# A decoder layer on one core: centred weights, heads on row halves, and low parts of the keys on GpSimd

## What is computed

```python
q, k, v = (x @ Wq.T), (x @ Wk.T), (x @ Wv.T)        # 16 heads of 16 features
mu = q.mean(-1); var = ((q - mu) ** 2).mean(-1)      # over the 16 features of a head; k alike
qn = (q - mu) / sqrt(var + 1e-5) * gamma + beta      # k alike
phi = [qn*qn / 4, sqrt(2/16) * qn_i * qn_j (i<j)]    # so phi_q . phi_k = (qn . kn / 4) ** 2
y = causal_sum(phi_q.phi_k * v) / (causal_sum(phi_q.phi_k) + 1e-5)
x = layernorm(x + y @ Wo.T)
```

## Time and profile before

| | us |
|---|---|
| median of 3 runs (lowest, highest) | 1490.67 (1488.88, 1492.04) |
| the profiled execution, its own time | 1501.86 |
| its span | 1500.1 |
| PE, DVE, POOL, ACT busy in the span | 1243.3, 754.2, 684.5, 582.5 |
| mean granted TensorE clock, share of full speed | 0.899 |

### The profile page before, as it was taken

The page is one execution under the profiler, slowest core; times in us unless marked ns, Lnnn a source line. Parts: engine busy times, 40 slices in busy tenths (PEclk is TensorE's granted clock), DMA queues, the critical chain, the costliest instruction groups (busy, mean ns, idle before and its releaser), DMA issues.

```text
span 1500.1 us, 20297 instructions
## 1 busy us (share of the span) xinstructions
PE 1243.3 (83%) x6416; PEld 712.3 (47%) x6416; DVE 754.2 (50%) x1328; ACT 582.5 (39%) x999; POOL 684.5 (46%) x597
## 2 busy tenths in 40 slices
PE   3488778856999899998999989999994449999970
PEld 3355454534554445544455444554543426666640
DVE  6475858536335753458624665446423432222217
ACT  3364555632444544445434444444441012222210
POOL 0132323420467674676655766666794431111111
PEclk8688897966999999999999999999996569999995
DMA  5580000010000100000000000000002921111113
GB/s 172 197 270 16 1 0 0 1 45 11 1 0 1 36 10 1 1 1 23 22 2 1 1 11 23 1 0 1 1 1 83 316 68 42 44 46 42 45 43 143
DMA packets 33007, 64.66 MB, mean 43 GB/s; under 512 B 4221, under 2 KB 22398, under 8 KB 32640
## 3 DMA queue, kind: packets, MB, share of 16 engines
q1 hardware_dynamic: 23200, 32.41, 6.6%
q10 hardware_dynamic: 6304, 22.59, 4.7%
q0 software_dynamic: 3408, 8.43, 1.6%
HBM read 52.89 MB, written 28.34 MB: 54 GB/s over the span
## 4 chain that ended last, share of the span: by engine, by line
PE 60%; DVE 20%; issue 10%; ACT 3%; POOL 2%; DMA 2%; another core or an unknown queue 1%; ACTq 1%; SPq 0%; DVEq 0%; POOLq 0%
PE PS L1582 11%; PE PS L1689 9%; PE PS L1510 9%; PE PS L1593 8%; DVE mxp L1168 5%; PE PS L1706 5%; PE PS L225 3%; PE PS L1417 2%; PE PS L1523 2%; PE PS L226 2%; PE PS L227 2%; DVE R L1148 2%; PE PS L1406 2%; PE PS L1427 2%; POOL acc L608 1%
## 5 line engine op out<-in xcount | busy, mean ns | idle before, releaser
L608 POOL TENSOR_TENSOR acc<-acc,PX 128x1024 f32<-128x1024 f32 (+1 forms) x176 | 421.2, 2393 | 161.1 <-ACT PX L846 155.2
L846 ACT ACTIVATE PX<-PS 128x1024 f32<-128x1024 f32 (+1 forms) x208 | 212.9, 1025 | 247.2 <-PE PS L1582 236.4
L1168 DVE TENSOR_REDUCE mxp<-PS 128x2 f32<-128x804 f32 x256 | 240.4, 986 | 132.3 <-PE PS L1523 131.9
L1593 PE MATMUL PS<-PX,V 128*64 128x512 f32 (+1 forms) x832 | 226.3, 623 | 0.0
L550 POOL TENSOR_SCALAR_AFFINE_SELECT A<-A 128x128 f32<-128x128 f32 x256 | 88.8, 359 | 219.8 <-ACT A L751 216.2
L1689 PE MATMUL PS<-W,XBT 128*128 x312 | 149.6, 603 | 1.3 <-ACT XBT L902 1.3
L751 ACT ACTIVATE A<-PS 128x512 f32<-128x512 f32 (+3 forms) x256 | 99.3, 437 | 98.0 <-PE PS L1417 90.9
L669 POOL DMA_INDIRECT Y<-yb,goal_u x39 | 38.4, 986 | 201.8 <-DVE yb L1327 196.7
L1417 PE MATMUL PS<-qT,kT 128*128 128x512 f32 (+3 forms) x256 | 88.0, 420 | 27.0 <-ACT A L751 21.9
L1582 PEld LDWEIGHTS PS<-QH,KH 64*128 64x128 f32 (+1 forms) x416 | 38.4, 181 | 151.3 <-issue 89.9
L1582 PE MATMUL PS<-QH,KH 64*128 64x512 f32 (+1 forms) x416 | 104.6, 499 | 3.5 <-issue 2.2
(11 more groups left out here) (261 smaller groups left out, 2138.9 us busy)
## 6 DMA issues: line engine op xcount, KB each, us to landing
W<-in_w SPq DMA_DIRECT2D x24, 512.0 KB
XB<-XG ACTq DMA_DIRECT2D x39, 129.0 KB, 2.1
yl<-Y SPq DMA_DIRECT2D x4, 1024.0 KB, 9.0
X<-in_x SPq DMA_DIRECT2D x1, 2048.0 KB, 12.1
out<-X SPq DMA_DIRECT2D x4, 512.0 KB, 2.9
xt_raw<-in_xt SPq DMA_DIRECT2D x3, 512.0 KB, 4.4
c_raw<-in_ctxt SPq DMA_DIRECT2D x6, 200.0 KB, 2.4
c_raw<-in_ctxt SPq DMA_DIRECT2D x12, 100.0 KB, 2.6
```

The source lines that it names most:

```text
L608: ins = pool.tensor_tensor(sums[0:r], sums[0:r], PX[0:r, (NL * p + t) % NP, :, :], ALU.add)
L846: act.activation(PX[0:r, u % NP, :, :], PS[0:r, score_buffer(u):score_buffer(u) + 2, :], ACT.Exp, scale=XD ** -0.5)\
L1168: dve.tensor_reduce(mxp[:, p % 2, :, v % NT, v // NT:v // NT + 1].rearrange("p a o -> p (a o)"), PS[:, k:k + 2, 0:BW], AX, ALU.max)\
L1593: mm = pe.matmul(PS[rows, 4, :], V[0:LROWS[j], j, P * p + XD * half:P * p + XD * half + XD], PX[0:LROWS[j], u % NP, half, :], start=(j == ...
```

## The change

1. The weights of q and k are centred once, in `raw`, before they are split: per head of 16 features the mean over the columns is taken off (DVE), so the projections come out centred and `centre` is gone from DVE. ACT squares straight from PSUM, and `normalise` reads PSUM and writes `cen`. Bank 2 is free only after `normalise` (`nrm_ok`). In the opening, odd blocks use bank 6.
2. `kT` holds two heads on 128 rows. A turn is one copy of 128x512, not two of 64x512. Scores are made in pairs: head 2m from rows 0 to 63, head 2m+1 from rows 64 to 127, into banks 4 and 5; ACT squares both in one instruction, and the next pair waits for that instruction. The memsets of `kT` are gone.
3. POOL makes the low parts of the keys; DVE keeps those of the queries.
4. Variance moves up to the slot of the squares, normalise and affine one slot earlier. On PE both projections of a block stand behind the slot's value products. The opening takes blocks in pairs.

```diff
-            for i in range(NT):
-                for after, kind in ((1, "project v"), (1, "project qk"), (2, "centre"), (3, "variance"), (4, "normalise"), (5, "affine")):
+            for i in reversed(range(NT)):
+                for after, kind in ((1, "project v"), (1, "project qk"), (2, "variance"), (2, "centre"), (3, "normalise"), (4, "affine")):
                     ahead.setdefault(2 * i + after, []).insert(0, (kind, i))
...
-        OPENING = [("x",)] + [(kind, 0) for kind in FEATURES[0:3]]
-        for i in range(NT):
-            OPENING += [(kind, i + 1) for kind in FEATURES[0:3] if i + 1 < NT] + [(kind, i) for kind in FEATURES[3:]] \
-                + ([("split", i - 1)] if i >= 1 else [])
-        OPENING += [("split", NT - 1)] + [("vs", g) for g in range(3)] \
+        OPENING = [("x",)]
+        for two in ((0, 1), (2, 3)):
+            OPENING += [(kind, i) for i in two for kind in FEATURES[0:3]] + [("variance", i) for i in two]
+            OPENING += [("split", i - 2) for i in two if i >= 2]
+            OPENING += [("normalise", i) for i in two] + [("affine", i) for i in two]
+        OPENING += [("split", i) for i in (2, 3)]
+        OPENING += [("vs", g) for g in range(3)] \
...
+                if s[0] == "split":
+                    i = s[1]
+                    k = feat[:, i, D:].rearrange("p (h f) -> p h f", f=SF)
+                    pool.wait_ge(hi_ok, 8 * b + 2 * i + 2)
+                    pool.tensor_tensor(KX[:, i, :, 1:4:2, :], k.unsqueeze(2).broadcast_to([P, SH, 2, SF]),
+                                       as32(KX[:, i, :, 0:4:2, :]), ALU.subtract).then_inc(lo_ok, 1)
...
-                act.wait_ge(cen_ok, NT * t + i + 1)
-                act.activation(feat[:, i, :], cen[:, i % 2, :], ACT.Square).then_inc(sq_ok, 1)
+                act.wait_ge(qk_mm, NT * t + i + 1)
+                act.activation(feat[:, i, :], bank(qk_bank(t, i)), ACT.Square).then_inc(sq_ok, 1)
...
-                for j in range(4):
-                    u, c = 4 * n + j, n % NT
-                    act.wait_ge(sc_mm, 64 * b + u + 1)
+                for two in range(2):
+                    u, c = 4 * n + 2 * two, n % NT
+                    act.wait_ge(sc_mm, 64 * b + u + 2)
...
-                    act.activation(A[:, u % 8, P * c:T], PS[:, 4 + u % 2, P * c:T], ACT.Square,
-                                   scale=0.25).then_inc(sqr_ok, 1)
+                    act.activation(A[:, u % 8:u % 8 + 2, P * c:T], PS[:, 4:6, P * c:T], ACT.Square,
+                                   scale=0.25).then_inc(sqr_ok, 2)
...
+            dve.wait_ge(ld_q, 16)
+            for c in range(KC):
+                ins = dve.tensor_reduce(w_mean[:, c, :], groups[c], AX, ALU.add)
+            ins.then_inc(wch, 1)
+            dve.wait_ge(wch, 1)
+            dve.tensor_scalar(w_mean[:, :, :], w_mean[:, :, :], -1.0 / SF, None, ALU.mult).then_inc(wch, 1)
+            dve.wait_ge(wch, 2)
+            for c in range(KC):
+                ins = dve.tensor_tensor(groups[c], groups[c], w_mean[:, c, :].unsqueeze(2).broadcast_to([P, 32, SF]), ALU.add)
...
-                chain(dve.tensor_reduce(g_mean[:, i % 2, :], v, AX, ALU.add), cch, at + 1)
-                chain(dve.tensor_scalar(g_mean[:, i % 2, :], g_mean[:, i % 2, :], -1.0 / SF, None, ALU.mult), cch, at + 2)
-                if wait:
-                    dve.wait_ge(feat_ok, NT * t + i - 1)
-                dve.tensor_tensor(cen[:, i % 2, :].rearrange("p (g f) -> p g f", f=SF), v,
-                                  g_mean[:, i % 2, :].unsqueeze(2).broadcast_to([P, 32, SF]), ALU.add).then_inc(cen_ok, 1)
...
-                dve.tensor_copy(kT[0:64, g % 2, 2 * q, :], bank(1, rows=64)).then_inc(kT_ok, 1)
-                dve.tensor_copy(kT[64:P, g % 2, 2 * q + 1, :], PS[64:P, 1, :]).then_inc(kT_ok, 1)
+                dve.tensor_copy(kT[:, g % 2, q, :], bank(1)).then_inc(kT_ok, 1)
...
-                if started(t, i, 1):
-                    pe.wait_ge(cen_ok, NT * t + i)
+                if isinstance(t, int) and t == 0:
+                    if i >= 2:
+                        pe.wait_ge(nrm_ok, i - 1)
+                else:
+                    pe.wait_ge(nrm_ok, NT * t + i)
...
-                if started(b, u, 2):
-                    pe.wait_ge(sqr_ok, 64 * b + u - 1)
-                pe.matmul(PS[:, 4 + u % 2, P * c:T], kT[:, g % 2, j, P * c:P * c + P],
-                          qT[:, g % 2, j // 2, P * c:T], start=True, stop=True).then_inc(sc_mm, 1)
+                if started(b, u, 2):
+                    pe.wait_ge(sqr_ok, 64 * b + u)
+                for half in range(2):
+                    rows = slice(64 * half, 64 * half + 64)
+                    pe.matmul(PS[:, 4 + half, P * c:T], kT[rows, g % 2, two, P * c:P * c + P],
+                              qT[rows, g % 2, two, P * c:T], start=True, stop=True).then_inc(sc_mm, 1)
...
-                    half = (len(steps) + 1) // 2
-                    for j in range(4):
+                    steps.sort(key=lambda ds: ds[1][0] in ("project qk", "project v"))
+                    half = min((len(steps) + 1) // 2, sum(s[0] not in ("project qk", "project v") for d, s in steps))
+                    for two in range(2):
```

More of the change, by code:

```diff
@@ L678, in _ @@
             act.dma_start(xt_raw[:, :, :], xt[0].rearrange("(c p) t -> p c t", p=P)).then_inc(ld_xt, 16)
-            act.wait_ge(ld_q, 16)
-            act.copy(WSh[:, :, 0:3 * D], raw[:, 0:2, 0:3 * D]).then_inc(w_hi, 1)
             def x_high(t):
@@ L765, in _ @@
                 if s == ("x",):
+                    act.wait_ge(wch, 3)
+                    act.copy(WSh[:, :, 0:3 * D], raw[:, 0:2, 0:3 * D]).then_inc(w_hi, 1)
                     act.wait_ge(ld_w, 16 * N_LDW)
@@ L934, in _ @@
             dve.memset(VS[:, :, :, SF:], 1.0).then_inc(const_dve, 1)
-            dve.memset(as32(kT[64:P, :, 0:4:2, :]), 0.0).then_inc(const_dve, 1)
-            dve.memset(as32(kT[0:64, :, 1:4:2, :]), 0.0).then_inc(const_dve, 1)
+            groups = [raw[:, c, 0:2 * D].rearrange("p (g f) -> p g f", f=SF) for c in range(KC)]
+            dve.wait_ge(ld_q, 16)
[7 more added lines that the diff above has]
+                ins = dve.tensor_tensor(groups[c], groups[c], w_mean[:, c, :].unsqueeze(2).broadcast_to([P, 32, SF]), ALU.add)
+            ins.then_inc(wch, 1)
+            dve.wait_ge(wch, 3)
             dve.wait_ge(w_hi, 1)
@@ L979, in normalise @@
                 v = cen[:, i % 2, :].rearrange("p (g f) -> p g f", f=SF)
-                dve.tensor_tensor(v, v, rs.unsqueeze(2).broadcast_to([P, 32, SF]), ALU.mult).then_inc(nrm_ok, 1)
+                if started(t, i, 2):
+                    dve.wait_ge(feat_ok, NT * t + i - 1)
+                dve.tensor_tensor(v, bank(qk_bank(t, i)).rearrange("p (g f) -> p g f", f=SF), rs.unsqueeze(2).broadcast_to([P, 32, SF]), ALU.mult).then_inc(nrm_ok, 1)
             def affine(t, i):
@@ L1373, in _ @@
             pe.wait_ge(const_pool, 3)
-            pe.wait_ge(const_dve, 3)
+            pe.wait_ge(const_dve, 1)
             pe.wait_ge(w_lo, 1)
@@ L1396, in project_v, with turn @@
                 mm.then_inc(v_mm, 1)
-            def turn(b, g, q, src, bk, done, free, per):
+            def turn(b, g, q, src, bk, done, free):
                 h = 4 * g + 2 * q
@@ L1403, in turn @@
                 if started(b, 2 * g + q, 1):
-                    pe.wait_ge(free, per * (8 * b + 2 * g + q))
+                    pe.wait_ge(free, 8 * b + 2 * g + q)
                 for i in range(NT):
@@ L1408, in turn, with scores @@
                 mm.then_inc(done, 1)
-            def score(b, n, j):
-                g, c, u = n // NT, n % NT, 4 * n + j
-                if c == 0 and j == 0:
+            def scores(b, n, two):
+                g, c, u = n // NT, n % NT, 4 * n + 2 * two
+                if c == 0 and two == 0:
                     pe.wait_ge(qT_ok, 8 * b + 2 * g + 2)
-                    pe.wait_ge(kT_ok, 16 * b + 4 * g + 4)
+                    pe.wait_ge(kT_ok, 8 * b + 2 * g + 2)
                 if started(b, u, 2):
-                    pe.wait_ge(sqr_ok, 64 * b + u - 1)
-                pe.matmul(PS[:, 4 + u % 2, P * c:T], kT[:, g % 2, j, P * c:P * c + P],
-                          qT[:, g % 2, j // 2, P * c:T], start=True, stop=True).then_inc(sc_mm, 1)
+                    pe.wait_ge(sqr_ok, 64 * b + u)
[3 more added lines that the diff above has]
+                              qT[rows, g % 2, two, P * c:T], start=True, stop=True).then_inc(sc_mm, 1)
             def value(b, n, j):
@@ L1448, in step @@
                 if kind == "turn q":
-                    turn(b, s[1], s[2], QX, 0, tq_mm, qT_ok, 1)
+                    turn(b, s[1], s[2], QX, 0, tq_mm, qT_ok)
                 if kind == "turn k":
-                    turn(b, s[1], s[2], KX, 1, tk_mm, kT_ok, 2)
+                    turn(b, s[1], s[2], KX, 1, tk_mm, kT_ok)
                 if kind == "back":
@@ L1476, in attention @@
```

(15 more changed lines are left out.)

23 lines of the change are left out of this document (8 added, 15 removed).

## The result

| | before | with the change |
|---|---|---|
| median, us (lowest, highest), 4 runs each | 1489.78 (1486.94, 1492.04) | 1528.97 (1523.49, 1531.24) |
| profiled execution, own time (span) | 1501.86 (1500.1) | 1523.49 (1521.7) |
| DVE, ACT, POOL busy | 754.2, 582.5, 684.5 | 701.6, 572.2, 693.6 |

The ratio is 1.0259, 95% interval [1.0225, 1.0292]: **slower by 39 us**, where 1496.5 was forecast with a range up to 1509. The sign was the one that held most of the chance; the size is out by a factor of over six.

A forecast was written before the change was run, and what follows sets the result against it. No engine was full; PE's waits in a ring of hand-overs bound the self-attention. Opening -1.5, batch 0 +1.9, loop batches +7.0 and batch 3 -1.5 gave +5.9 on the profiled 1501.9, carried over to 1496.5 us; range 1475 to 1509.

The forecast's parts named there:

- The sum, batch 2 at full clock: Self-attention batch 2, added by stretches of slots: 69.3 us, 2.3 less than before; with low clock 75.1, 3.5 more.
- Low keys on POOL: Slots 9 to 12: subtraction takes 1.3 us, masks come 1.3 to 2 later, all but about 1 us a batch hidden.
- Scores in pairs: Self-attention scores: PE's score work halves, paired rounds cost 1.02 us of square plus 0.6 latency; batch 3 gains 1.5.
- the waits for bank 2: PE in slots 3, 5 and 7 waits for normalise before the next projection: 3.1, 3.2 and 4.1 us.
- The lower clock behind them: Projections after those waits run at half clock: 1.75 us more each, 5.8 a loop batch with half an output projection.
- The opening: Before the first batch: PE starts at 14, first turn comes at 46.6 instead of 48.09, saving 1.5 us.
- what would show it: Right: nine 3 to 4 us waits, lower clock, batches 73 or more. Wrong: slots 10 to 13 waiting over 1 for masks.
- POOL is slow: Rival, 0.10: POOL's low part takes 2.6 us and delays masks; +6 to +12 on top, 1502 to 1509.
- the root on ACT: Slots 3, 5, 7: ACT takes the previous block's root only after its squares, then DVE's chain takes 1.9 us.
- The clock holds: Rival, 0.28: projections of slots 3, 5 and 7 run at 2.4 GHz; loop batches win 2.3 each, 1480.
- Waits cancel: Rival, 0.16: ACT reaches its root earlier, each batch loses 2 us less of waiting; 1491.
- Row halves bring nothing: Rival, 0.03: paired 64-row score matmuls are drained or run in series; +18 on top, 1514.

The follow-up runs named there:

- r2: The changed kernel, but DVE copies the projection to `cen` at once, freeing bank 2 early; square and normalise read the copy: 1494.57 us, ratio 1.0031.
- r8: The kernel before with row halves alone (one `kT` copy a turn, 64-row scores), each head squared singly: 1488.01 us, ratio 0.9991.
- r5: r4 with the low keys back on DVE: 1472.41 us, ratio 0.9893 to the kernel before.
- r1: The changed kernel with the low keys on DVE again, behind those of the queries: 1517.87 us, ratio 1.0182 to the kernel before.
- r6: The kernel before with the low keys on POOL and nothing else changed: 1500.57 us, ratio 1.009.
- r4: The changed kernel with the edits of r2 and r3 together: 1481.06 us, ratio 0.9939 to the kernel before.
- r3: The changed kernel, row halves kept, but each head scored and squared by itself in two banks by turns: 1515.11 us, ratio 1.017.
- r16: r5 run again unchanged, on the chip of the job of r13 and r14: 1472.36 us, ratio 0.989 to the kernel before.
- r7: The changed kernel with ACT taking the root ahead of the squares of its slot: 1538.44 us, ratio 1.0343 to the kernel before.
- r9: r7 with DVE also normalising ahead of the copy of a finished group: 1513.88 us, ratio 1.0109 to the kernel before.
- r13: r16 plus POOL's low-key subtraction on spare buffers, same shape and place, result unused: 1491.63 us, ratio 1.0032 to the kernel before.
- r14: r16 plus five masks of 128x128 on a spare buffer at the subtraction's place on POOL: 1488.05 us, ratio 1.0004 to the kernel before.
- r10: r4 with POOL's low-key subtraction behind the masks of the next slot: 1490.48 us, ratio 0.9932 to the kernel before.

## Why the prediction was right and wrong

In short: the waits came as forecast, and the forecast failed in what it set against them and in two costs that it put near nothing. The steps that failed are the 69.3 us of "The sum, batch 2 at full clock", the 1 us a batch of "Low keys on POOL", and the -1.5 of batch 3 by "Scores in pairs".

**Right: the waits for bank 2.** Nine, of 2.94, 3.04 and 3.98 us in batch 1 against 3.1, 3.2 and 4.1; in batch 0, 3.06, 2.20 and 3.06. The lower clock behind them, and its price per projection (1.55 to 1.85 in the loop batches for 1.75), were right too. The opening was right: first turn at 45.63 for 46.6. So were a period over 73 us and a lower granted clock, of "what would show it"; but one of its signs of being wrong came as well, in slot 10 alone: value products waiting 1.43 to 1.49 us for masks in each of batches 0 to 2.

**Wrong: the list, "The sum, batch 2 at full clock".** It has 69.3 us (its five stretches add to 69.4) with waits of 10.4 in it, so it counts on 12.7 us of gains under the 71.6 of before. r2 takes the waits away, and its loop batches still need 72.1 and 71.3. The gains set against the waits (DVE 14.4 us lighter, scores on half the rows) did not pay as the list had it: r8 shows no change for row halves and single copies, and r5, with the three harmful parts undone, wins some 4 and 7 us a loop batch. The waits were sized right and charged for the most part: they are 28.1 us, the low clock behind eight of them some 13 more by the lengths of the projections (an estimate), and r2 gives back 34.4. It is 12.6 and 10.7 us shorter than the changed kernel in batches 1 and 2, and 6.9 in batch 0, where +1.9 was forecast. By stretches of batches 1 and 2 (with the list's low clock of 1.75 per projection): 0 to 3 were 15.4 and 13.8 for 13.0; 3 to 5, 14.4 and 15.5 for 13.9; 5 to 8, 24.3 and 22.4 for 21.4; 8 to 13, 20.5 and 20.3 for 17.2; 13 to 0, 10.1 twice for 9.2. The largest steady miss is slots 8 to 13, and there it is the next point.

**Wrong: "Low keys on POOL", about 1 us a batch.** It cost 11 us by r1, 12 by r6, 9 from r4 to r5; some 3 to 4 a batch. The duration was near (1390 ns for 1300). What failed is "ACT's rounds hide all but about 1 us": the list put the masks 1.3 to 2 us later, and in slot 10 they start 2.5 us after the last square, half of it the wait for ACT's rounded keys, which stands in POOL's queue ahead of masks that are due. With r1 the stretch of slots 8 to 13 is 2.5 and 3.3 us shorter. The rival "POOL is slow" named a price (+6 to +12) near this one for a reason that did not come, a low part of 2.6 us; that is luck.

**Wrong: "Scores in pairs" and batch 3, -1.5.** It came to +4.5, and pairing costs 14 us by r3. The forecast names the bank that PE can no longer refill beside ACT, but puts no price on losing it: its list gives batch 3 43.2 us with pairs, which is what r3 takes without them. The round itself was right at full clock. ACT's squares of 256 columns in batch 3 of the changed kernel start 317.44 - 316.29 = 1.15 apart, 0.60 of it square, where the list had 1.2:

```profile
316.29 0.60 ACT L761 ACTIVATE A<-PS 128x512 f32<-128x512 f32 x1 [0.61 <-PE PS L1429]
317.44 0.60 ACT L761 ACTIVATE A<-PS 128x512 f32<-128x512 f32 x1 [0.55 <-PE PS L1429]
```

What it was set against was wrong: singly, in two banks by turns, the same two heads take 0.90 us, by PE's timeline of r16,

```profile
267.60 0.39 PE L1434 MATMUL PS<-qT,kT 64*128 64x256 f32 x2
268.50 0.61 PE L1434 MATMUL PS<-qT,kT 64*128 64x256 f32 x2
```

because PE fills one bank while ACT reads the other. In pairs ACT waits 0.55 us for PE in such a round, singly 0.24; and at the low clock the round of 512 columns takes 2.08, where the list has 1.62. A second slip is the base: 44.7 was the width of a window; by the anchors the batch took 43.3 before, so even the list's 43.2 was no gain.

**Wrong in its mechanism: the root on ACT.** The prediction's price for slots 3, 5 and 7 rests on ACT taking the root behind its squares. In slot 7 it named the copy and the layer norm on DVE as well, and in slot 5 the statistics; for slot 3 it named nothing on DVE. There the copy of the finished group ends at 148.92 and the root at 148.85, so the two ways tie and 3.1 for 2.94 is in part luck. r7 and r9 show DVE's queue to be what holds: with the root early, alone, slot 3 still waits 2.87 us and the whole is 9.5 us slower; with normalise ahead of the copy 2.6 us are left of all nine waits.

**Rivals.** "The clock holds" is refused by the rows at 0.43 apart, in eight projections of nine, "Waits cancel" by 28.1 us of waiting, "Row halves bring nothing" by r8 as to harm, though row halves do bring nothing.

The parts as measured, in ratios turned into us of 1490 and undone one after another: the wait for bank 2 34, pairs 14 (from r2 to r4), low keys on POOL 7 (from r4 to r5), the rest -16. As steps of one path they add up to the 39 by construction; that the first two are separate is shown by r4. What stays open: how far the memory access shared with DVE takes part in the price of the low keys, as r13 and r14 both have it and their intervals overlap; why r10's gain is in its trace and not in its median; and how much of the 34 is clock and how much the wait itself (for the projections three times 1.85, 5.5 us a loop batch, is the upper end that the rows support; the rest of PE's work at the low clock was not separated).

## What to carry to other kernels

A step that is moved onto an in-order queue brings its own wait along: ask what is queued behind it and who waits for that, before you ask how long it takes. Here the copies taken off an engine with slack brought nothing that shows (r8), while a buffer that is held through one more engine's queue was paid for the most part, with the clock on top; a copy of 0.7 us that frees the bank bought back 34. And where two banks alternated, joining their two readers into one instruction lost the overlap and cost 14 us (r3).

## What was unexpected of the hardware

Beside POOL's strided subtraction DVE's low part of the keys, of two SBUF inputs, went from 732 to 1020 ns in r13, and two such operations from 692 and 711 to 871 and 888 on average in the changed kernel, while POOL's own took 1390 for 1286 beside the attention. Beside POOL's masks it stayed at 750, but there the masks stretch: five in a row took 1.7 to 2.6 us, not 5 x 0.294, the longest while DVE ran three such operations. Scores of 64 rows instead of 128 changed the time by -0.1 per cent, [-0.3, +0.1], and PE kept showing the low clock for whole slots after a wait (batch 3, 0.78 for 0.92) although no wait there was over 1.2 us.
